# Attention and gated feed-forward on one core: when the query stacks and weight loads of the first two pairs are issued

## The reference

```python
x = x + xattn(layernorm(x), ctx, ctx, Wq, Wk, Wv, Wfc, bfc)   # 32 heads of 16, 8 groups of keys and values
x = x + ffn(layernorm(x), w_gating, w_linear)                 # fp8 operands, hidden size 2048

score = einsum('bhqd,bhkd->bhqk', qh, kh) / 4
attn = softmax(score)
out = einsum('bhqk,bhkd->bhqd', attn, vh) @ Wfc.T + bfc
ffn = (gelu(x @ w_gating[0]) * (x @ w_gating[1])) @ w_linear
```

## Time and profile before

| what | value |
|---|---|
| median of three runs | 449.24 us |
| profiled execution | 447.77 us, span 446.0 us |
| TensorE busy | 420.6 us, 94% of the span |
| VectorE, ScalarE, GpSimd busy | 330.7, 313.2, 237.2 us |
| mean granted clock of TensorE | 0.984 of full speed |
| first transposed score of pair 0, of pair 1 | 29.98 us, 60.70 us from the start of the span |
| one loop from pair 2 on | about 50 us |

### The profile page before, as it was taken

How to read it: one execution, slowest core, us unless ns; L and a number is a source line. 1 busy time by engine, 2 the same in 40 slices (tenths; PEclk the granted TensorE clock), 3 DMA queues, 4 the chain that set the end, 5 groups by cost and what they waited for, 6 DMA issues and landing times.

```text
span 446.0 us, 11827 instructions
## 1 busy us (share of the span) xinstructions
PE 420.6 (94%) x4620; PEld 342.6 (77%) x4620; DVE 330.7 (74%) x709; ACT 313.2 (70%) x579; POOL 237.2 (53%) x228
## 2 busy tenths in 40 slices
PE   6968878989989999999999999999999999999997
PEld 5856556878967779877897789878887789657983
DVE  4686878578958579975997679975997679577442
ACT  5848849867897645888479755987479755895541
POOL 4398888966447613586328823685328823462000
PEclk9998998999989999999999999999999999999999
DMA  7987981478622551034701543034601342000001
GB/s 243 326 212 259 300 209 53 123 215 255 208 92 67 172 129 41 1 91 124 167 5 33 159 114 80 2 87 137 160 3 38 86 105 64 3 25 26 1 27 47
DMA packets 21287, 50.06 MB, mean 112 GB/s; under 512 B 4688, under 2 KB 5200, under 8 KB 21200
## 3 DMA queue, kind: packets, MB, share of 16 engines
q1 hardware_dynamic: 21054, 48.89, 38.6%
q10 hardware_dynamic: 178, 0.41, 0.4%
HBM read 23.86 MB, written 4.19 MB: 63 GB/s over the span
## 4 chain that ended last, share of the span: by engine, by line
PE 78%; DVE 10%; ACT 3%; issue 3%; POOL 2%; DMA 2%; SPq 0%; DVEq 0%; ACTq 0%; POOLq 0%
PE bank L731 21%; PE bank L753 11%; PE bank L515 8%; PE bank L516 7%; PE bank L517 7%; PE bank L596 6%; PE bank L627 6%; DVE mneg L1204 3%; PE bank L550 3%; PE bank L651 3%; PE bank L653 2%; PE bank L561 2%; PE bank L667 1%; DMA cin<-in_ctx 1%; DVE osum L1222 1%
## 5 line engine op out<-in xcount | busy, mean ns | idle before, releaser
L1443 POOL TENSOR_TENSOR plo<-p,phi 128x512 f16<-128x512 f32 x124 | 143.9, 1169 | 61.5 <-ACT phi L945 60.5
L731 PE MATMUL bank<-x2T,wgate 128*128 128x128 fp8e4 x2048 | 123.8, 219 | 0.8 <-DVE xr L1287 0.5
L731 PEld LDWEIGHTS bank<-x2T,wgate 128*128 128x128 fp8e4 x2048 | 115.6, 98 | 11.6 <-issue 8.5
L1204 DVE TENSOR_REDUCE mneg<-bank 128x4 fp32r<-128x512 f32 x128 | 84.0, 685 | 12.9 <-PE bank L596 12.9
L942 ACT ACTIVATE p<-bank 128x512 f32<-128x512 f32 x124 | 75.0, 605 | 24.9 <-PE bank L627 24.2
L945 ACT ACTIVATE phi<-bank 128x512 f16<-128x512 f32 x128 | 77.3, 604 | 0.0
L753 PE MATMUL bank<-wlin,act 128*128 128x512 fp8e4 x256 | 71.5, 381 | 0.0
L964 ACT ACTIVATE gate<-bank 128x512 bf16<-128x512 f32 x64 | 38.3, 598 | 39.3 <-PE bank L731 38.2
L968 ACT CAST ff<-bank 128x512 bf16<-128x512 f32 x64 | 37.5, 586 | 34.7 <-PE bank L731 34.4
L627 PE MATMUL bank<-qs,ks 98*128 98x512 f32 x128 | 55.6, 434 | 3.0 <-DMA qs<-mrow 2.5
L596 PE MATMUL bank<-kmask,cq 128*128 128x512 f32 x128 | 51.8, 457 | 6.7 <-DVE mneg L1204 3.7
(11 more groups left out here) (114 smaller groups left out, 820.6 us busy)
## 6 DMA issues: line engine op xcount, KB each, us to landing
qs<-cq SPq DMA_DIRECT2D x93, 128.0 KB, 2.4
stage<-in_w SPq DMA_DIRECT2D x22, 512.0 KB, 5.0
ks<-khl SPq DMA_DIRECT2D x96, 64.0 KB, 2.0
xr<-in_x SPq DMA_DIRECT2D x16, 256.0 KB, 3.9
cin<-in_ctx SPq DMA_DIRECT2D x8, 512.0 KB, 4.1
out<-xr SPq DMA_DIRECT2D x16, 256.0 KB, 2.7
kmask<-khl SPq DMA_DIRECT2D x28, 64.0 KB, 2.2
raw<-in_w SPq DMA_DIRECT2D x3, 512.0 KB, 7.6
```

The lines of the kernel that those rows point to most:

```text
L731: mm = pe.matmul(out[:, h * SEQ:(h + 1) * SEQ], wgate8[:, UH * v + h, kk, part, :], x2T[:, b % ABUF, kk, :], start=kk == 0, stop=kk == KT - 1)
L1204: dve.tensor_reduce(dst[:, :, 2 * half:2 * half + 2, j].rearrange("p a r -> p r a"), bank_of("S", q, i, s)[:, :].rearrange("p (r a k) -> p ...
L1443: pool.tensor_tensor(plo[:, e % PBUF, :], p32[:, pool_tiles(e) % P32BUF, :], phi[:, e % PBUF, :], ALU.subtract).then_inc(plo_ok, 1)
```

## The change

SP's program alone is changed, in the stretch that serves pairs 0 and 1. For pair 0, SP waits until the first row of maxima (which ACT sends) has landed before it issues the query stacks of group pairs 2 and 3 and what follows them. For pair 1, the key stacks go ahead of the loads of x and of weight chunks, the row of maxima of pair 1's first batch goes behind the query stacks of one group pair in place of two, and chunks 12 to 16 are all loaded behind the last query stack, in place of three ahead of the key stacks and two at the end.

```diff
             for hp in range(PAIRS):
                 stack_k(0, hp)
-            for hp in range(1, PAIRS):
+            stack_q(0, 1)
+            sp.wait_ge(m_stacked[0], 16)
+            for hp in range(2, PAIRS):
                 stack_q(0, hp)
             copy_select()
             for c in range(7, 12):
...
             mask_k(1)
             stack_max(0, 1)
             load_ctx(2)
-            load_x(2)
-            for c in range(12, 15):
-                load_chunk(c)
             for hp in range(PAIRS):
                 stack_k(1, hp)
-            for hp in range(PAIRS // 2):
+            load_x(2)
+            stack_q(1, 0)
+            stack_max(1, 0)
+            for hp in range(1, PAIRS):
                 stack_q(1, hp)
-            stack_max(1, 0)
-            for hp in range(PAIRS // 2, PAIRS):
-                stack_q(1, hp)
-            load_chunk(15)
-            load_chunk(16)
+            for c in range(12, 17):
+                load_chunk(c)
```

## The result

The changed kernel took 450.71 us in the median of 20 runs (447.66 to 453.84), the kernel before 447.58 us in 20 runs beside it (444.04 to 450.34). The ratio is 1.0082, 95% interval 1.0059 to 1.0105: slower by 0.8%, 3.6 us between the means. I had forecast no change to speak of. The runs also scatter somewhat more (standard deviation 2.0 us against 1.7).

The account below looks back on a forecast made before the run. TensorE holds 78% of the chain; POOL and DVE set parts of the stretch from 26 to 75 us. Terms 0, +0.2, 0 and -0.4 gave -0.2: 447.6 us profiled, forecast put at 448.5, range 445.9 to 450.9.

Parts of the forecast that it names:

- Step 1: Pair 0's first row lands at 29.0 us; TensorE's first transposed score 1.0 us earlier (0 to 1.45), worth 0.
- best case: Pair 0's first row lands at 28.53 us: batch 1's 2.28 us counted from ACT's issue at 26.25.
- Rival B: Pair 0's scores, 32 to 36 us: earlier start keeps TensorE's clock up, -0.9 to -1.3 us; chance 0.17.
- Rival D: Pair 0's first row still lands at 29.9 us, behind ACT's own copies; 447.8 to 449.3 us; chance 0.12.
- Step 2: SP's copies behind pair 0's wait: stacks and chunks slip, hidden by slack; masks and batch 1's row cost +0.2 us.
- +0.2, bounds 0 and +1.0: Masks and batch 1's row at 44.56 and 45.38 us: 0 if engines catch up, +1.0 if they follow late chunks.
- Rival C: Masks and batch 1's row queue behind delayed chunks on SP: slower by 1.0 to 1.5 us; chance 0.18.
- slower by over 1%: Whole kernel slower by more than 4.5 us: chance 0.04, against 0.93 for within 1%.
- Step 3: Pair 1's row lands earlier, second pair's first score gains 0.9 us (0.5 to 0.94), hidden behind DVE's maximum: worth 0.
- the offset: Profiled execution lies 1.5 us below the three-run median, 449.24; added to the profiled forecast it gives 449.0.
- The -0.4 us for a better clock: Whole-kernel allowance in the sum for TensorE keeping its full clock when pair 0's scores start earlier.

Follow-up runs that it names:

- ACT's masks: Pair 1's four mask copies issued by ACT in place of SP, with the wait in pair 0, against the kernel before: 1.0084; without the wait 1.0066.
- wait alone: Kernel before with only pair 0's wait for the first row, pair 1's order unchanged: 1.0045, and 1.0058 when run a second time.
- key stacks back: Changed kernel with pair 1's key stacks back behind the loads of x and chunks 12 to 14, against the kernel before: 1.0076.
- held until masks: Changed kernel with SP waiting until the masks have landed before issuing the context and key stacks, against the kernel before: 1.0101.
- The row alone: Kernel before with only pair 1's row of maxima moved behind one group pair's stacks in place of two: 1.0002.
- the transposes: Kernel before with nine unused transposes of the identity on TensorE ahead of the first transposed score: 1.0022.

## Why the prediction failed, step by step
**Step 1, the wait.** Right in kind, a little large in size. From ACT's issue to TensorE's first transposed score, the eight profiles without the wait show 3.4 to 4.3 us (3.73 in the earlier trace rows), nine of the ten with it 3.2 to 3.4 (the tenth, with ACT's masks, 4.1): the row comes about 0.7 us earlier, I had said 1.0. My best case was too good: it put SP's 2.28 us for batch 1's row, which hold 0.74 of issuing, behind a start of ACT's issuing that takes 1.20. And it is worth nothing on the chain, as predicted: the kernel with the wait and chunks 9 to 11 behind the masks has the earlier row and 1.0007 [0.9987, 1.0026]. Rival B didn't come either: the changed kernel's profile is at half clock for 6.8 us between 32 and 40. Rival D is out in its strict form. Its thought was half right, though. In the changed kernel, the DMA engines stood nearly still for the last microsecond before the row landed at 31.25 (stretch, busy, clock, DMA share, GB/s):
```profile
30.00:31.00 1.00, 0.00 (x0) 1.00 0.07 16
```
So at least the last microsecond of the row's time is not spent behind other transfers.

**Step 2, what is queued behind the wait. This is the step that failed**, in its term for the masks: "+0.2, bounds 0 and +1.0". The query stacks, the selecting rows and chunk 8 were hidden as worked out; no wait for them appears before 90 us in either profile of the changed kernel. The chunks slipped by 2.2 to 2.7 us, as I said (2.5). The masks then came late by a size that changes from run to run, with TensorE's wait at 1.1, 1.2, 2.0, 2.1, 3.0 and 4.5 us in the six profiles that have the wait in pair 0 and all five chunks ahead of SP's masks, where the kernel before has 0.6. It goes with the lead that chunk 11's issue has over the first mask's: 3.6, 3.3, 3.5, 3.1, 1.8 and 2.1 us in the same order, against 5.6. Up to 1.3 us nothing is lost, since the row of batch 1 is waited for anyway. From 2.0 us on, scores 7 to 12 of pair 0 take 10.5 to 14.0 us in place of 8.5 to 8.8:

| kernel, one profile each | wait for masks, us | scores 7 to 12, us |
|---|---|---|
| before | 0.6 | 8.54 |
| changed | 1.1 | 8.55 |
| wait alone, second | 1.2 | 8.59 |
| key stacks back | 2.0 | 10.48 |
| wait alone | 2.1 | 10.83 |
| held until masks | 3.0 | 11.48 |
| changed, second | 4.5 | 14.04 |
| wait, chunks 9 to 11 behind | 0.6 | 8.64 |

Over the six the loss in the table is 2.1 us in the mean, less than the 2.4 us (wait alone) and 3.7 us (changed kernel) of all runs, so this place holds the greater part of the loss but isn't shown to hold all of it.

Two errors made the bound too low. First, I shifted chunk 11's 8.0 us as they stood and let the masks follow at once. But 8.0 is one execution's value of a thing that varies: it was 7.4 to 10.3 in the profiles with the wait, and the masks landed 0.8 to 1.9 us behind it. Second, I priced the wait and not what comes behind it. In the profile of the wait alone, score 8 is 1.0 us further from score 7, and scores 8 to 11 then take 5.97 in place of 4.57 us at half clock: the clock adds 1.4 us to a wait that cost 1.0. In the second profile of the changed kernel it is 3.6 us and 2.3 us. The Trainium skill (TensorE: Matmul & The Clock Gate, What's actually happening) says that the throttled clock is the default and activity releases it; the trace agrees, with the granted clock at 1.00 from 46 to 47 and at 0.50 when TensorE starts again at 48.53 after 4.3 us without work. I had this rule in mind for rival B only, as a gain.

Rival C, with the right place, got 0.18 and at most 1.5 us. The mean was 3.6 us. It named SP's queue as the reason, and the masks on ACT's queue speak against that part. That I gave slower by over 1% only 0.04 still holds, barely: the loss is 0.8%.

**Step 3, pair 1.** Right in what it is worth, where the parts could be seen. The row alone gives 1.0002 [0.998, 1.0024] and all of pair 1's order 1.0014 [0.9991, 1.0036]. The gain at the place itself was too large, 0.9 us. In the changed kernel's profile the second pair's first score comes 0.3 us earlier, counted from the score before it. I had TensorE's last product end at 59.8, but in the kernel before it still had three matmuls of the output projection, the last at
```profile
60.21 0.39 PE L517 MATMUL bank<-wfc,aoT 128*128 128x512 f32 x1
```
so only some 0.3 us were to be had before 60.70. It makes no difference: DVE's maximum follows at the same distance. In the changed kernel's profile the wait for that maximum is
```profile
67.09 0.29 PEld L595 LDWEIGHTS bank<-kmask,cq 128*128 128x128 f32 x1 [2.71 <-DVE mneg L1203]
```
against 2.59 us. What pair 1's order adds when the wait is there as well, about 1.3 us, I can't explain; both mechanisms that I proposed fell.

**The sum and the offset.** The forecast of 448.5 came from four executions between 445.87 and 450.34. Over 20 runs the kernel before has its median at 447.58, so the base was 0.9 us too high. That hid a part of the miss: against the right base I had forecast about zero and the kernel lost 3.6 us. The measured median, 450.71, lies inside my range of 445.9 to 450.9, but by luck: it reaches so far up only by its allowance for the scatter of a few runs and by the base that was too high, and no case in it held a loss of 3 us. (Its stated parts, 448.5 + 1.5 + 1.3, would even give 451.3.) The -0.4 us for a better clock also came out the other way: the mean granted clock fell.

## What to carry to other kernels
When a wait is put ahead of a batch of large loads, look at what small and urgent transfer is issued behind these loads by something that the wait doesn't delay: the loads then slide into it, and another queue for the small one did not help here. Order transfers by due time, with large loads that aren't wanted yet behind the small copies that are wanted now; here that move made the wait free. And a bound for a transfer's landing needs more than the one value in the trace, with the half-clock stretch that a long stand brings counted as part of its price.

## What the runs showed of the hardware
- A 512 KB load issued last of five took 7.4 to 10.3 us to land over these profiles (7.5 to 8.5 in those without the wait). In the wait alone it landed at 44.6, with TensorE still waiting for the masks until 46.4. The microsecond around that landing had a mean share of the DMA engines of only 0.16:
```profile
44.00:45.00 1.00, 0.53 (x5) 1.00 0.16 50
```
A low mean share doesn't mean that the transfer that matters is through.
- Two profiles of one kernel differ by 1.4 to 2.6 us at pair 0's score 9 (three kernels profiled twice), and those of two kernels by 1.8 us at 24 us, before anything differs in the program. One profile of each kernel could not have shown this effect.
- A copy of 64 KB within SBUF, issued while large loads are under way, is as late on the other issuing engine's queue: medians of 4.0 us on ACT's queue against 3.9 and 4.4 on SP's, where it took 2.4 on either with the loads further ahead.
- Time at half clock isn't lost one for one: the execution with 3 us of it in the first 180 us (with the transposes) took 447.18 us, the one with 17 us (the kernel before, again) 449.08. Over the kernel before's runs it is 0.2 to 0.3 us for each microsecond.
